# First attention: TensorE's turns issued ahead of its scores; the other attentions fetch q and k by head group

## The chip, the cores and the metric

The kernel runs on one core of a Trainium2 chip. The metric is the device time of one execution in microseconds (us), the median of the runs. All inputs are float32 and lie in the chip's memory at the start; the result must lie there at the end.

## The reference, cut to what matters

A transformer stack of four layers over an input of 4 sequences x 512 tokens x 256 features. Each layer is an attention and a feed-forward part (SwiGLU, a spline lookup, latent experts, experts with a top-2 router):

```
x = x + _L0_attn_ref(_layernorm(x), ...)   # windowed mask, ALiBi, rotary, 8 key/value heads
x = x + _L0_ffn_ref(_layernorm(x), ...)
x = x + _L1_attn_ref(_layernorm(x), ...)   # causal
x = x + _L1_ffn_ref(_layernorm(x), ...)
x = x + _L2_attn_ref(_layernorm(x), ...)   # causal, rotary
x = x + _L2_ffn_ref(_layernorm(x), ...)
x = x + _L3_attn_ref(_layernorm(x), ...)   # no mask
x = x + _L3_ffn_ref(_layernorm(x), ...)
```

Every attention has 16 heads of 16 dimensions: scores q k^T of 512 x 512 for each head and sequence, a softmax over keys, the product with v, and an output projection. The change touches the four attentions alone.

## The kernel before, in words

`build` runs eight stages one after the other, with a barrier between them. `PS` is PSUM, 8 banks of 512 float32 on 128 partitions. SyncE (SP) issues the DMAs, GpSimd (POOL) does small elementwise work.

**The first attention** is `attention_window`. It walks over FULL = 128 steps: 4 sequences (b) x 4 groups of four heads (g) x 2 halves x 4 query blocks of 128. Here a step is called N. On each engine the program is a Python loop over N that was unrolled, so the order in the code is the order on the engine. In step N:

- `scores(N)` (TensorE, L592): two matmuls, one for each of two heads, 128 queries x 448 keys, into banks 2(N mod 2) and 2(N mod 2)+1. It waits for the exponentials of step N-2, since these read the same two banks.
- `minima(N)` (VectorE, L361): for each of the two heads it adds the distance bias in PSUM and takes the row's minimum (the scores are negated).
- `exponentials(N)` (ScalarE, L492): for each of the two heads, exp with that minimum, into the buffer `p`.
- `turn_weights(e)` (TensorE, L602) for the two items e = 2(N-9) and 2(N-9)+1: each item is four 128x128 transposes of `p` of nine steps ago, into bank 4 or 5 (4 + e mod 2). It waits until item e-2 has been copied out of the same bank.
- `keep_turned(e)` copies that bank to `pT`. ScalarE does it (L500), and VectorE for every fifth item (L370, e mod 5 = 2). It stands behind `exponentials(N)` on ScalarE and behind `minima(N)` on VectorE.
- `piece(...)`: in 21 of 32 steps one piece of other work that uses bank 7: layer-norm turns (L556), projections of the next sequence (L568), turning a finished group (L623), turning heads (L630), output projections (L640). The table `plan` says which.
- `values(J)` (TensorE, L616) in every even step from 12 on: probabilities times v, four matmuls.

The last scores are those of step 127; 13 more steps only turn and multiply.

**The other three attentions** are `attention_quads`. q and k are projected with the heads side by side. To spread each head's 16 dimensions over the partitions they go through a buffer in the chip's memory, `spread_scratch`: `store_unit(b, u)` writes unit u (u = 0: q of the head groups 0 and 1, 1: k of the groups 0 and 1, 2 and 3: the same for the groups 2 and 3) in three DMAs of 256 KB, and `fetch_unit(b, u)` reads it back into `q` or `k` in two DMAs of 512 KB, 64 partitions each (L866). The semaphore `spread[u]` counts them. All stand on SP in the order store 0, store 1, fetch 0, fetch 1, store 2, store 3, fetch 2, fetch 3. TensorE's `scores(t)` (L1200) is the first reader: it computes scores for the row maxima only (VectorE, L975), 16 tiles for each group of heads, and it waits before a tile that is the first of groups 0 and 1, or of 2 and 3, until both units have landed. The first attention already fetches by group (L256, L259): four DMAs of 192 KB for each group.

Of the kernel before, what the change touches and what calls it, by code (L numbers as in the profile page):

```python
# [5 lines left out]
F32 = mybir.dt.float32  # L6
# [11 lines left out]
TB = S // P  # L18
# [5 lines left out]
NG = H // GH  # L24
# [94 lines left out]
def attention_window(nc, tag, X, cst, PS, scr, weights, rope, scale, dist, slopes, bias):  # L119
# [4 lines left out]
    NU = 3  # L124
    WC = 2 * (D + VD)
    STEPS = 2 * TB * NG
    FULL = NB * STEPS
# [4 lines left out]
    with ExitStack() as ctx:  # L132
# [3 lines left out]
        sem = ctx.enter_context(stage_semaphores(nc, tag))  # L136
# [9 lines left out]
        q, k = sb("q", [P, RING, 2, S], R32), sb("k", [P, RING, 2, S], R32)  # L146
# [19 lines left out]
        wrote = [sem(f"wrote{u}") for u in range(NU)]  # L166
        spread = [sem(f"spread{g}") for g in range(NG)]
# [15 lines left out]
        def piece_at(N):  # L183

            kind, ahead, i = plan.get(N % STEPS, ("none", 0, 0))
            b = N // STEPS + ahead
            return (kind, b, i) if 0 <= b < NB else ("none", 0, 0)

        def previous_piece(N):
            return next((x for x in (piece_at(n) for n in range(N - 1, -1, -1)) if x[0] != "none"), ("values", 0, 0))  # L190
# [29 lines left out]
        with nc.Block() as block:  # L220
# [325 lines left out]
            def _(pe):  # L546
# [35 lines left out]
                def scores(N):  # L582
                    b, n = N // STEPS, N % STEPS
                    g, half, qt = n // 8, n % 8 // TB, n % TB
                    slot = (NG * b + g) % RING
                    if n % 8 == 0:
                        pe.wait_ge(spread[g], 64 * (b + 1))
                    if N >= 2:
                        pe.wait_ge(exp_done, 2 * (N - 1))
                    for a in range(2):  # L590
                        rows = slice(64 * a, 64 * a + 48)
                        pe.matmul(PS[:, 2 * (N % 2) + a, 0:KW], q[rows, slot, half, qt * P:(qt + 1) * P],  # L592
                                  k[rows, slot, half, GLOB:S], start=True, stop=True).then_inc(s_done, 1)

                def turn_weights(e):

                    gg, kt, i = e // (4 * GH), e % (4 * GH) // GH, e % GH
                    pe.wait_ge(exp_done, 16 * gg + (8 if i < 2 else 16))
                    if e >= 2:
                        pe.wait_ge(*turned_item(e - 2))  # L600
                    for qt in range(TB):
                        mm = pe.transpose(PS[:, 4 + e % 2, qt * P:(qt + 1) * P],  # L602
                                          p[:, GH * (gg % 2) + i, qt, kt * P:(kt + 1) * P], ident)
                    mm.then_inc(pt_done, 1)
# [39 lines left out]
                def piece(kind, b, i, before):  # L644
                    if kind == "none":
                        return
                    pe.wait_ge(*freed(before))
                    if kind == "group":
                        turn_group(b, i)
                    elif kind == "turn":  # L650
                        turn(b, i, 7)
                    elif kind == "project":
                        project(b, i, 7)
                    elif kind == "values":
                        values_of(b)
                    elif kind == "heads":
                        turn_heads(b, i)
                    else:
                        outputs(b, i)
# [16 lines left out]
                pe.wait_ge(xT_done, 2 * KC)  # L676
                pe.wait_ge(sin_done, NU)
                for N in range(END):
                    if N < FULL:
                        scores(N)  # L680
                    for e in (2 * (N - LAG), 2 * (N - LAG) + 1):
                        if 0 <= e < ITEMS:
                            turn_weights(e)
                    piece(*piece_at(N), previous_piece(N))
                    if N % 2 == 0 and 0 <= (N - 12) // 2 < ITEMS // GH:
                        values((N - 12) // 2)
# [7 lines left out]
def attention_quads(nc, tag, X, Y, cst, PS, scr, filled, weights, masks=None, rope=None, bias=None, scrambled=False):  # L694
# [4 lines left out]
    NU = 4  # L699
# [5 lines left out]
    STEPS = 2 * TB * NG  # L705
    TILES_ = 2 * STEPS
    LEAD = 24
    FULL = NB * STEPS
    SCALE = HD ** -0.5
    with ExitStack() as ctx:  # L710
# [3 lines left out]
        sem = ctx.enter_context(stage_semaphores(nc, tag))  # L714
# [34 lines left out]
        unit_high = [sem(f"unit_high{u}") for u in range(NU)]  # L749
        unit_low = [sem(f"unit_low{u}") for u in range(NU)]  # L750
        wrote = [sem(f"wrote{u}") for u in range(NU)]
        spread = [sem(f"spread{u}") for u in range(NU)]
        v_done, va_done = sem("v_done"), sem("va_done")
        s_done, max_done, split_done = sem("s_done"), sem("max_done"), sem("split_done")
        m_done, mT_done, ma_done, mb_done = sem("m_done"), sem("mT_done"), sem("ma_done"), sem("mb_done")
# [72 lines left out]
        with nc.Block() as block:  # L828
            @block.sync
            def _(sp):  # L830
                o = KC * WC
                sp.wait_ge(filled, 16 * 2 * NU)
                if bias is not None:
                    sp.dma_start(bb[:, :], bias.rearrange("(a n) -> a n", a=1).broadcast_to([P, D])
                                 ).then_inc(loaded_bias, 16)
                sp.dma_start(wqk_in, weights[:, 0:o]).then_inc(loaded_qk, 16)
                if rope is not None:
                    sp.dma_start(tabs[:, :, :].rearrange("p a b -> p (a b)"), rope[:, :]).then_inc(loaded_tab, 16)
                sp.dma_start(wv_in, weights[:, o:o + KC * D]).then_inc(loaded_v, 16)
                if causal:  # L840
                    sp.dma_start(masks_in, masks[:, :]).then_inc(loaded_masks, 16)
                sp.dma_start(wo[:, :, :].rearrange("p a b -> p (a b)"),
                             weights[:, o + KC * D:o + KC * D + NC * D]).then_inc(loaded_o, 16)

                def store_unit(b, u):

                    par = b % 2
                    if b >= 2:
                        sp.wait_ge(spread[u], 32 * (b - 1))
                    sp.wait_ge(unit_high[u], b + 1)  # L850
                    for place in ((0, 1) if u % 2 else (0, 3)):
                        sp.dma_start(scr[par, u, place, :, :, :].rearrange("d l c -> (d l) c"),
                                     high[:, u, :].bitcast(F32)).then_inc(wrote[u], 16)
                    sp.wait_ge(unit_low[u], b + 1)
                    sp.dma_start(scr[par, u, 3 if u % 2 else 1, :, :, :].rearrange("d l c -> (d l) c"),
                                 low[:, u, :].bitcast(F32)).then_inc(wrote[u], 16)

                def fetch_unit(b, u):

                    par = b % 2  # L860
                    sp.wait_ge(wrote[u], 48 * (b + 1))
                    if b >= 2 and u == 0:
                        sp.wait_ge(st_done, STEPS * (b - 1))
                    dst = k if u % 2 else q
                    for a in range(2):
                        sp.dma_start(dst[64 * a:64 * a + 64, par, 4 * (u // 2):4 * (u // 2) + 4, :].bitcast(F32),  # L866
                                     scr[par, u, :, :, 4 * a:4 * a + 4, :].rearrange("k d l c -> (k d) l c")
                                     ).then_inc(spread[u], 16)

                for b in range(NB):  # L870
                    store_unit(b, 0)
                    store_unit(b, 1)
                    fetch_unit(b, 0)
                    fetch_unit(b, 1)
                    store_unit(b, 2)
                    store_unit(b, 3)
                    fetch_unit(b, 2)
                    fetch_unit(b, 3)

            @block.gpsimd  # L880
            def _(pool):
# [274 lines left out]
            def _(pe):  # L1156
# [32 lines left out]
                def scores(t):  # L1189

                    gg, qt, half, a = tile_of(t)
                    b, g = gg // NG, gg % NG
                    pair, kw, rows = 2 * g + half, (qt + 1) * P if causal else S, slice(64 * a, 64 * a + 64)
                    if t % (8 * TB) == 0:
                        pe.wait_ge(spread[g // 2 * 2], 32 * (b + 1))
                        pe.wait_ge(spread[g // 2 * 2 + 1], 32 * (b + 1))
                    if t >= 2:
                        pe.wait_ge(max_done, t - 1)
                    ps = PS[:, 4 + a, :]
                    mm = pe.matmul(ps[:, 0:kw], q[rows, b % 2, pair, qt * P:(qt + 1) * P], k[rows, b % 2, pair, 0:kw],  # L1200
                                   start=True, stop=not causal)
                    if causal:
                        pe.matmul(ps[:, kw - P:kw], half_masks[rows, 0, 0, :], half_masks[rows, 1, 0, :],  # L1203
                                  start=False, stop=False)
                        mm = pe.matmul(ps[:, kw - 64:kw], half_masks[rows, 0, 1, :], half_masks[rows, 1, 1, 64:P],  # L1205
                                       start=False, stop=True)
                    mm.then_inc(s_done, 1)
# [1310 lines left out]
```

## Time and profile before

| | us |
|---|---|
| median of 3 runs | 2176.14 |
| lowest and highest run | 2170.74, 2186.18 |
| the profiled execution | 2171.83 |
| its span in the trace | 2170.0 |
| TensorE busy | 1694.2 (78%) |
| VectorE busy | 1176.7 (54%) |
| ScalarE busy | 937.5 (43%) |
| GpSimd busy | 365.6 (17%) |
| DMA | 138.86 MB, 64 GB/s over the span |

The span is the time from the first to the last instruction of the trace; 1.83 us of the execution lie outside it. Busy times of engines overlap, and no engine is busy all the time, so where the time goes is read stage by stage, from the timeline and from what ended each wait. The first attention lies from 46 to 449 us of the span; the first score matmuls of the other three attentions start at 644.3, 1087.6 and 1684.3 us.

### The profile page before, as it was taken

To read this page: it belongs to the slowest core of one execution; us is meant where nothing else is said; L and a number is where in the kernel's file an instruction comes from. 1 tells how busy PE (TensorE), PEld (TensorE's weight loads), DVE (VectorE), ACT (ScalarE), POOL (GpSimd) and SP (SyncE) were. 2 spreads that over 40 slices of the span, in tenths; PEclk is the share of its full clock that TensorE was granted. 3 is DMA by queue.
4 is the path that set the end of the run, shared out by engine and by line. 5 is a ranking of instruction groups with operands and counts; after the bars stand their busy time and mean duration, and the time that the engine had idled before them with its cause. 6 is when DMAs were issued, how large, how long until landed. Compare 5 with 4: busy or idle time off the path is not lost. (4 is left out here: it accounts for less than half of the span.)

```text
span 2170.0 us, 30921 instructions
## 1 busy us (share of the span) xinstructions
PE 1694.2 (78%) x11334; PEld 1050.3 (48%) x11342; DVE 1176.7 (54%) x2681; ACT 937.5 (43%) x1452; POOL 365.6 (17%) x466
## 2 busy tenths in 40 slices
PE   3889898859968999801389999579996899997676
PEld 2445454548855555501255555356665344443543
DVE  2566656543235665489556656242223677774555
ACT  1667778733223544400124445233332356564422
POOL 4120200012323212020322230000001412200000
PEclk8799999989977999955669999769998799999588
DMA  6232230010044335010334541100003345220101
GB/s 206 55 75 55 59 85 4 1 58 0 0 141 108 95 94 137 1 45 0 110 104 105 137 116 22 67 0 0 0 0 91 103 105 136 71 66 22 45 0 39
DMA packets 49297, 138.86 MB, mean 64 GB/s; under 512 B 7169, under 2 KB 12682, under 8 KB 42130
## 3 DMA queue, kind: packets, MB, share of 16 engines
q1 hardware_dynamic: 49170, 137.17, 23.3%
q8 instruction: 80, 1.31, 0.3%
q14 instruction: 47, 0.39, 0.1%
HBM read 87.86 MB, written 51.38 MB: 64 GB/s over the span
## 5 line engine op out<-in xcount | busy, mean ns | idle before, releaser
L975 DVE TENSOR_REDUCE a_mx<-PS 128x1 f32<-128x512 f32 (+3 forms) x768 | 395.9, 554 | 208.8 <-PE PS L1205 132.3
L1146 ACT ACTIVATE a_pT<-PS 128x1024 f32<-128x1024 f32 (+3 forms) x384 | 308.0, 810 | 217.0 <-PE PS L1229 149.3
L1200 PE MATMUL PS<-a_k,a_q 64*128 64x512 f32 (+3 forms) x768 | 236.2, 443 | 59.0 <-DMA a_k<-spread_scratch 28.8
L361 DVE CUSTOM_DVE_ANT_0 PS<-PS,a_dist 128x448 f32<-128x448 f32 x256 | 155.0, 649 | 89.2 <-PE PS L592 88.3
L1220 PE MATMUL PS<-a_q,a_k 64*128 64x512 f32 (+3 forms) x768 | 177.9, 448 | 14.8 <-DVE a_q L980 6.1
L602 PE MATMUL PS<-cst,a_p 128*128 128x128 f32 x1024 | 146.9, 286 | 50.5 <-ACT a_pT L500 45.9
L492 ACT ACTIVATE a_p<-PS,a_negm 128x448 f32<-128x448 f32 (+1 forms) x256 | 152.7, 633 | 77.2 <-DVE a_negm L361 76.4
L1243 PE MATMUL PS<-a_pT,a_va 128*32 128x512 f32 (+3 forms) x1536 | 170.2, 516 | 5.7 <-ACT a_raw L1102 5.7
L1200 PEld LDWEIGHTS PS<-a_k,a_q 64*128 64x128 f32 x768 | 112.5, 202 | 104.6 <-DVE a_mx L975 66.8
L602 PEld LDWEIGHTS PS<-cst,a_p 128*128 128x128 f32 x1024 | 113.4, 145 | 87.2 <-ACT a_p L492 60.7
L1220 PEld LDWEIGHTS PS<-a_q,a_k 64*128 64x128 f32 x768 | 78.8, 192 | 111.1 <-issue 82.7
L500 ACT ACTIVATE a_pT<-PS 128x512 f32<-128x512 f32 x205 | 114.0, 599 | 9.0 <-PE PS L602 8.2
L1918 DVE SCALAR_TENSOR_TENSOR f_acc<-PS,f_gb,f_acc 128x128 f32<-128x128 f32 x144 | 40.6, 345 | 115.5 <-PE PS L2018 115.4
L1954 ACT ACTIVATE f_hid<-PS,f_b 128x512 f32<-128x512 f32 x84 | 57.7, 687 | 77.3 <-PE PS L2009 75.5
L1080 ACT ACTIVATE a_q<-PS 16x1024 fp32r<-16x1024 f32 x48 | 48.7, 1014 | 96.0 <-PE PS L1251 95.6
L1203 PE MATMUL PS<-a_half_masks 64*128 64x128 bf16 x512 | 90.0, 243 | 0.0
L2018 PEld LDWEIGHTS PS<-f_w,f_hid 128*128 128x128 f32 x672 | 80.1, 192 | 15.3 <-issue 14.3
L2009 PE MATMUL PS<-f_lat,f_w 128*128 128x512 f32 x168 | 82.8, 608 | 0.0
L2018 PE MATMUL PS<-f_w,f_hid 128*128 128x128 f32 x672 | 80.2, 275 | 0.0
L592 PE MATMUL PS<-a_k,a_q 48*128 48x448 f32 x256 | 62.9, 489 | 14.8 <-DMA a_k<-window_scratch 9.7
L1205 PE MATMUL PS<-a_half_masks 64*128 64x64 bf16 x512 | 74.4, 200 | 0.0
L1174 PE MATMUL PS<-a_xnT,a_w_highqk 128*128 128x512 f32 x128 | 58.8, 459 | 17.1 <-DVE a_x_low L1029 9.4
(337 smaller groups left out, 3262.9 us busy)
## 6 DMA issues: line engine op xcount, KB each, us to landing
spread_scratch<-a_high SPq DMA_DIRECT2D x96, 256.0 KB, 2.5
a_q<-spread_scratch SPq DMA_DIRECT2D x48, 512.0 KB, 6.6
a_k<-spread_scratch SPq DMA_DIRECT2D x48, 512.0 KB, 9.3
spread_scratch<-a_low SPq DMA_DIRECT2D x48, 256.0 KB, 3.9
window_scratch<-a_high SPq DMA_DIRECT2D x24, 256.0 KB, 2.2
a_q<-window_scratch SPq DMA_DIRECT2D x32, 192.0 KB, 5.3
a_k<-window_scratch SPq DMA_DIRECT2D x32, 192.0 KB, 6.2
window_scratch<-a_low SPq DMA_DIRECT2D x12, 256.0 KB, 2.0
```

The lines of the kernel that those rows point to most:

```text
L361: dve.tensor_tensor_reduce(PS[:, bank, 0:KW], PS[:, bank, 0:KW], dt_[:, off:off + KW], float(slopes[2 * pair + a]), 3e38, ALU.add, ALU.min ...
L492: act.activation(p[p0:P, GH * (gg % 2) + i, qt, 0:KW], PS[p0:P, bank, 0:KW], ACT.Exp, bias=negm[p0:P, bank:bank + 1], scale=-1.0).then_inc ...
L500: act.activation(pT[:, J % 2, i, :], PS[:, 4 + e % 2, :], ACT.Copy).then_inc(turned_act, 1)
L602: mm = pe.transpose(PS[:, 4 + e % 2, qt * P:(qt + 1) * P], p[:, GH * (gg % 2) + i, qt, kt * P:(kt + 1) * P], ident)
L975: dve.tensor_reduce(mx[:, gg % 2, qt, 2 * half + a:2 * half + a + 1], PS[:, 4 + a, 0:kw], AX.X, ALU.max).then_inc(max_done, 1)
L1146: act.activation(pT[:, N // 2 % 2, N % 2, :, q0:S], PS[:, 2 * (N % 2):2 * (N % 2) + 2, q0:S], ACT.Exp, scale=SCALE).then_inc(exp_done, 1)
L1200: mm = pe.matmul(ps[:, 0:kw], q[rows, b % 2, pair, qt * P:(qt + 1) * P], k[rows, b % 2, pair, 0:kw], start=True, stop=not causal)
L1203: pe.matmul(ps[:, kw - P:kw], half_masks[rows, 0, 0, :], half_masks[rows, 1, 0, :], start=False, stop=False)
L1220: mm = pe.matmul(PS[:, 2 * half + a, q0:S], k[rows, b % 2, pair, kt * P:(kt + 1) * P], q[rows, b % 2, pair, q0:S], start=True, stop=not ca ...
L1243: mm = pe.matmul(PS[BLK * i:BLK * i + BLK, 6, q0:S], va[:, b % 2, kt, GH * g + i, :], pT[:, J % 2, i // 2, i % 2, q0:S], start=(kt == 0), ...
L2009: pe.matmul(PS[:, n % 2, :], w1[:, n, :], lat[:, :], start=True, stop=True).then_inc(h_done, 1)
L2018: mm = pe.matmul(PS[:, 2 + e % 2, k * P:(k + 1) * P], hid[:, e % 2, j, k * P:(k + 1) * P], w2[:, first[e] + j, :], start=(j == 0), stop=(j ...
```

## The change

On TensorE in `attention_window`, the two turns of a step now stand ahead of its scores. No instruction is added or removed there. In `attention_quads`, q and k are fetched by group of heads: four DMAs of 256 KB for each group in place of two of 512 KB for each unit; the groups 0 and 1 are fetched when both units 0 and 1 are in the scratch buffer, and TensorE waits for one group at a time.

```diff
@@ attention_window, tensor
                 for N in range(END):
-                    if N < FULL:
-                        scores(N)
                     for e in (2 * (N - LAG), 2 * (N - LAG) + 1):
                         if 0 <= e < ITEMS:
                             turn_weights(e)
+                    if N < FULL:
+                        scores(N)
                     piece(*piece_at(N), previous_piece(N))
@@ attention_quads
-        spread = [sem(f"spread{u}") for u in range(NU)]
+        spread = [sem(f"spread{g}") for g in range(NG)]
@@ store_unit
                     if b >= 2:
-                        sp.wait_ge(spread[u], 32 * (b - 1))
+                        for g in (u // 2 * 2, u // 2 * 2 + 1):
+                            sp.wait_ge(spread[g], 64 * (b - 1))
@@
-                def fetch_unit(b, u):
-
-                    par = b % 2
-                    sp.wait_ge(wrote[u], 48 * (b + 1))
-                    if b >= 2 and u == 0:
-                        sp.wait_ge(st_done, STEPS * (b - 1))
-                    dst = k if u % 2 else q
+                def fetch_group(b, g):
+
+                    par, tile = b % 2, g // 2 * 2
+                    if g % 2 == 0:
+                        sp.wait_ge(wrote[tile], 48 * (b + 1))
+                        sp.wait_ge(wrote[tile + 1], 48 * (b + 1))
+                    if b >= 2:
+                        sp.wait_ge(st_done, STEPS * (b - 2) + 8 * (g + 1))
                     for a in range(2):
-                        sp.dma_start(dst[64 * a:64 * a + 64, par, 4 * (u // 2):4 * (u // 2) + 4, :].bitcast(F32),
-                                     scr[par, u, :, :, 4 * a:4 * a + 4, :].rearrange("k d l c -> (k d) l c")
-                                     ).then_inc(spread[u], 16)
+                        first = 4 * a + 2 * (g % 2)
+                        for u, dst in ((tile, q), (tile + 1, k)):
+                            sp.dma_start(dst[64 * a:64 * a + 64, par, 2 * g:2 * g + 2, :].bitcast(F32),
+                                         scr[par, u, :, :, first:first + 2, :].rearrange("k d l c -> (k d) l c")
+                                         ).then_inc(spread[g], 16)
@@ attention_quads, tensor, scores(t)
-                    if t % (8 * TB) == 0:
-                        pe.wait_ge(spread[g // 2 * 2], 32 * (b + 1))
-                        pe.wait_ge(spread[g // 2 * 2 + 1], 32 * (b + 1))
+                    if t % (4 * TB) == 0:
+                        pe.wait_ge(spread[g], 64 * (b + 1))
```

In the program that this makes, TensorE's order in the first attention changes in every step from 9 to 127. Before, at a place in the first sequence (L602 turns, L592 scores, L616 values, L623 and L630 pieces):

```order
L616 MATMUL PS<-a_pT,a_va 32x512 x4
L592 MATMUL PS<-a_k,a_q 128x448 x2
L602 MATMUL PS<-cst,a_p 128x128 x8
L592 MATMUL PS<-a_k,a_q 128x448 x2
L602 MATMUL PS<-cst,a_p 128x128 x8
L623 MATMUL PS<-cst,a_raw 128x128 x4
L616 MATMUL PS<-a_pT,a_va 32x512 x4
```

Now, on TensorE at the same place:

```order
L616 MATMUL PS<-a_pT,a_va 32x512 x4
L602 MATMUL PS<-cst,a_p 128x128 x8
L592 MATMUL PS<-a_k,a_q 128x448 x2
L602 MATMUL PS<-cst,a_p 128x128 x8
L592 MATMUL PS<-a_k,a_q 128x448 x2
L623 MATMUL PS<-cst,a_raw 128x128 x4
L616 MATMUL PS<-a_pT,a_va 32x512 x4
```

The scores of a step moved behind its eight transposes; pieces and values keep their places.

On SP, at the start of each of the other attentions, the order before was (L852 and L855 stores, L866 fetches):

```order
L852 DMA spread_scratch<-a_high 128x512 x2
L855 DMA spread_scratch<-a_low 128x512
L866 DMA a_q<-spread_scratch 64x2048 x2
L866 DMA a_k<-spread_scratch 64x2048 x2
L852 DMA spread_scratch<-a_high 128x512 x2
L855 DMA spread_scratch<-a_low 128x512
```

And on SP now (L853 and L856 are the same stores, L870 the fetches):

```order
L853 DMA spread_scratch<-a_high 128x512 x2
L856 DMA spread_scratch<-a_low 128x512
L870 DMA a_q<-spread_scratch 64x1024
L870 DMA a_k<-spread_scratch 64x1024
L870 DMA a_q<-spread_scratch 64x1024
L870 DMA a_k<-spread_scratch 64x1024
L870 DMA a_q<-spread_scratch 64x1024
L870 DMA a_k<-spread_scratch 64x1024
L870 DMA a_q<-spread_scratch 64x1024
L870 DMA a_k<-spread_scratch 64x1024
L853 DMA spread_scratch<-a_high 128x512 x2
L856 DMA spread_scratch<-a_low 128x512
```

Eight half-size fetches stand where four stood; the first four of them are group 0.

## Rows read from the trace of the kernel before

**Rows 1.** Page, costliest groups: line engine op x count | busy, mean ns | idle before, releaser.

```profile
L361 DVE CUSTOM_DVE_ANT_0 PS<-PS,a_dist 128x448 f32<-128x448 f32 x256 | 155.0, 649 | 89.2 <-PE PS L592 88.3
...
L602 PE MATMUL PS<-cst,a_p 128*128 128x128 f32 x1024 | 146.9, 286 | 50.5 <-ACT a_pT L500 45.9
L492 ACT ACTIVATE a_p<-PS,a_negm 128x448 f32<-128x448 f32 (+1 forms) x256 | 152.7, 633 | 77.2 <-DVE a_negm L361 76.4
```

**Rows 2.** Timeline of TensorE, 232 to 238 us: start, us, engine line op.

```profile
232.09 0.47 PE L592 MATMUL PS<-a_k,a_q 48*128 48x448 f32 x2
232.49 1.09 PE L602 MATMUL PS<-cst,a_p 128*128 128x128 f32 x8
233.52 0.47 PE L592 MATMUL PS<-a_k,a_q 48*128 48x448 f32 x2
235.17 1.12 PE L602 MATMUL PS<-cst,a_p 128*128 128x128 f32 x8 [1.19 <-ACT a_pT L500]
236.12 0.60 PE L630 MATMUL PS<-cst,a_at 128*128 128x128 f32 x4
236.65 1.07 PE L616 MATMUL PS<-a_pT,a_va 128*32 128x512 f32 x8
237.65 0.47 PE L592 MATMUL PS<-a_k,a_q 48*128 48x448 f32 x2
```

**Rows 3.** Timeline of VectorE and ScalarE, the same stretch.

```profile
232.60 0.63 DVE L361 CUSTOM_DVE_ANT_0 PS<-PS,a_dist 128x448 f32<-128x448 f32 x1 [0.68 <-PE PS L592]
...
233.32 1.21 ACT L492 ACTIVATE a_p<-PS,a_negm 128x448 f32<-128x448 f32 x2 [1.13 <-DVE a_negm L361]
234.44 1.08 ACT L500 ACTIVATE a_pT<-PS 128x512 f32<-128x512 f32 x2
235.39 1.17 ACT L492 ACTIVATE a_p<-PS,a_negm 128x448 f32<-128x448 f32 x2
```

**Rows 4.** Timeline of TensorE: scores and turns of steps 9 and 10.

```profile
72.47 0.74 PE L592 MATMUL PS<-a_k,a_q 48*128 48x448 f32 x2 [0.35 <-ACT a_p L492]
73.15 1.97 PE L602 MATMUL PS<-cst,a_p 128*128 128x128 f32 x8
75.05 0.74 PE L592 MATMUL PS<-a_k,a_q 48*128 48x448 f32 x2
```

**Rows 5.** Timeline of TensorE: the scores of step 127, the last.

```profile
418.92 0.47 PE L592 MATMUL PS<-a_k,a_q 48*128 48x448 f32 x2
```

**Rows 6.** Timeline of VectorE in step 10, TensorE at the lower clock.

```profile
75.82 0.63 DVE L361 CUSTOM_DVE_ANT_0 PS<-PS,a_dist 128x448 f32<-128x448 f32 x1 [1.26 <-PE PS L592]
```

**Rows 7.** Windows: stretch, busy of PE PEld DVE ACT POOL, clock, DMA share, GB/s.

```profile
46.00:72.00 26.00, 13.09 (x34) 5.53 (x34) 14.48 (x41) 11.05 (x20) 12.57 (x16) 0.63 0.58 136
...
73.00:82.00 9.00, 8.91 (x39) 7.29 (x38) 4.71 (x15) 7.20 (x13) 0.00 (x0) 0.50 0.00 0
...
330.00:420.00 90.00, 73.05 (x518) 43.35 (x517) 54.08 (x158) 70.60 (x130) 0.00 (x0) 1.00 0.00 1
```

**Rows 8.** Waits: who waited for whom, us in total, times, longest.

```profile
PE PS L1200 <- DMA a_k<-spread_scratch: 28.8, 3, 10.5
```

**Rows 9.** Timeline of SP and TensorE at the start of the second attention.

```profile
631.56 1.13 SPq L866 DMA_DIRECT2D a_q<-spread_scratch  x2
633.97 1.08 SPq L866 DMA_DIRECT2D a_k<-spread_scratch  x2
...
644.30 0.80 PE L1200 MATMUL PS<-a_k,a_q 64*128 64x512 f32 x2 [9.39 <-DMA a_k<-spread_scratch]
```

**Rows 10.** The first attention's start: first fetch issued by SP, first scores.

```profile
39.06 0.33 SPq L256 DMA_DIRECT2D a_q<-window_scratch  x1
...
46.01 0.74 PE L592 MATMUL PS<-a_k,a_q 48*128 48x448 f32 x2 [9.73 <-DMA a_k<-window_scratch]
```

**Rows 11.** Page, DMA issues: KB each, median us from issue to landing.

```profile
a_q<-spread_scratch SPq DMA_DIRECT2D x48, 512.0 KB, 6.6
a_k<-spread_scratch SPq DMA_DIRECT2D x48, 512.0 KB, 9.3
```

More of the change, by code:

```diff
@@ L872, in _ @@
                     store_unit(b, 1)
-                    fetch_unit(b, 0)
-                    fetch_unit(b, 1)
+                    fetch_group(b, 0)
+                    fetch_group(b, 1)
                     store_unit(b, 2)
                     store_unit(b, 3)
-                    fetch_unit(b, 2)
-                    fetch_unit(b, 3)
+                    fetch_group(b, 2)
+                    fetch_group(b, 3)
             @block.gpsimd
```

## The prediction

> **What bounds the kernel now.** I read the stage table of the timeline first: eight stages with barriers, so each edit pays only in its own stage, and nothing can pass from one stage to the next. Then the costliest groups: in the first attention ScalarE sat idle 77.2 us ahead of its exponentials, ended nearly always by VectorE's minima; VectorE sat idle 89.2 us ahead of the minima, ended by the scores; TensorE sat idle 50.5 us ahead of the turns, ended by ScalarE's copies of earlier turns [rows 1]. No engine is full; they wait for one another in a ring. So the question is the ring's length, and that is read from the timeline of one pair of steps.
>
> An even step starts with its scores at 232.09 and its turns at 232.49; the odd step's scores follow at 233.52, at once. The odd step's turns wait 1.19 us for ScalarE's copies and start at 235.17; then come a piece (236.12), the values (236.65) and the next even step's scores at 237.65 [rows 2]. On the other engines: minima from 232.60, exponentials from 233.32, copies of the turns from 234.44, and the odd step's exponentials from 235.39, without idle time, since its scores had been issued early [rows 3]. Two steps took 237.65 - 232.09 = 5.56 us, 2.78 a step. What the reader is to see: the odd step's scores stand ahead of the turns that wait, so the way scores, minima, exponentials of one step runs beside the way copies, turns of the step before. That overlap is what makes 2.78 possible.
>
> Over the whole stage, the scores of step 9 (the first step with turns) start at 72.47 [rows 4], and those of step 127, the last, at 418.92 [rows 5]: 346.4 us for 118 steps, 2.94 each.
>
> **The change, part one: turns ahead of scores.** It adds and removes no instruction. Follow the waits in the new order. The turns of step N+1 go to banks 4 and 5 and wait until the turns of step N are copied out. ScalarE's copies of step N stand behind its exponentials of step N. Those need the minima of N, these the scores of N, and the scores of N now stand behind the turns of N on TensorE, which works in order. So turns, scores, minima, exponentials, copies, turns of the next step form one ring, with a single step in it, and nothing overlaps. Its length, link by link, at the full clock:
>
> - scores' start to minima's start: 232.60 - 232.09 = 0.51 [rows 2, 3]
> - minima's start to exponentials' start: 233.32 - 232.60 = 0.72 [rows 3]
> - exponentials' start to the copies' start: 234.44 - 233.32 = 1.12 [rows 3]
> - copies' start to the next turns' start (the first copy must be out, the second follows while the first item is turned): 235.17 - 234.44 = 0.73 [rows 2, 3]
> - turns' start to the next instruction of TensorE, now the scores: 236.12 - 235.17 = 0.95 [rows 2]; where the turns do not wait in between, it is about 1.03, as 233.52 - 232.49 shows.
>
> The sum is 4.03 us. I take 0.1 off (3.92): one item in five is copied by VectorE, which is free by then, and where that is the first of a pair, in one step of five, ScalarE's own copy is over some 0.45 us sooner (by the 1.08 us of two copies, which pipeline, against 0.60 for one). What else a step does is hidden in this ring: TensorE is idle from the end of the scores, about 0.4 us after their start, until the turns, 0.51 + 0.72 + 1.12 + 0.73 = 3.08 us after their start; a piece like L630 (0.53 us, 236.65 - 236.12) and the values (1.00 us, 237.65 - 236.65) fit [rows 2]. A projection and the values together fill it about exactly; I give that nothing. ScalarE's and VectorE's pieces fall into waits of 1.7 us and more.
>
> So 118 steps x 3.92 = 462.6 us at the full clock. The first nine steps have no turns and the last thirteen no scores: unchanged.
>
> **The clock.** At the start of this stretch TensorE ran at 1.2 GHz: the granted clock was 0.50 from 73 to 82 us while TensorE was busy 8.91 of 9 us [rows 7]; from 330 to 420 us it was 1.00 at 73.05 busy us of 90 [rows 7]. A step at 1.2 GHz: turns to next scores take 75.05 - 73.15 = 1.90 instead of 0.95 to 1.03 [rows 4], scores to minima 75.82 - 75.05 = 0.77 instead of 0.51 [rows 4, 6]. The new ring holds both in full: 3.92 + 0.9 + 0.26 is about 5.2 us with a little more for the second copy's wait, 1.3 more a step. Before, the lower clock lasted about ten microseconds of the stretch after step 9, four steps. Busy time per step stays (73.05 us in 90 is 2.26 a step at 2.78), so the busy share falls from 0.81 to 2.26 / 3.92 = 0.58. The nearest stretch with so little is 46 to 72 us: busy 13.09 of 26, clock 0.63 [rows 7], but that has waits of several us, where here no idle gap is over 2.7. I take 12 steps of 118 at the lower clock: 12 x 1.3 = 16 us. Ends: 4 steps (5 us) and all of them (153 us).
>
> Here a rule speaks against the change. By the Trainium skill ("TensorE: Matmul & The Clock Gate", Part 4, on transposes by TensorE), transposes do not count as activity for the clock the way other matmuls do. The row from 73 to 82 us, where only turns and scores ran and the clock stayed at 0.50, agrees. By that rule the activity that counts would be thinner still in the new order, and the all-low end of the range nearer; that is the clock rival below.
>
> Sum of part one: 462.6 + 16 - 346.4 = +132 us.
>
> **Part two: fetch by group.** TensorE waited for k's landing three times, once at each of the other attentions' starts, 28.8 us in all [rows 8]; in later sequences it never did, so only the starts can gain. In the second attention q's fetches were issued at 631.56, k's at 633.97, and the scores began at 644.30 [rows 9], 10.3 us after k's issue. Now nothing is issued before both units are stored, so q's head start of 2.4 us goes, and four DMAs of 256 KB are issued from 633.97 on. The nearest case is the first attention's: its first fetch of group 0 (four DMAs, 768 KB in all) was issued at 39.06 and the scores began at 46.01, 6.95 us later [rows 10]. With 1 MB I take 7.7 us (0.75 more for the further 256 KB, at the rate of the fetches there), so 641.7 in place of 644.3: 2.6 us for each attention, 8 us for three. Ends: nothing (the eight DMAs of both groups share the engines, and group 0 lands with group 1), and 12 us. Group 1 has 16 tiles' time to land; the stores of units 2 and 3 stand behind four more issues, about 2.2 us later by 1.13 us for two [rows 9], and their readers come 32 tiles later.
>
> A DMA of 512 KB landed after 6.6 to 9.3 us at the median [rows 11]. The Trainium skill ("DMA: Bandwidth & Descriptors", Bandwidth) advises DMAs of 1 MiB and more, so halving them would cost bandwidth. By that rule part two could be worth nothing; the first attention's start shows that several small DMAs in flight together land quickly, so I keep 8.
>
> **Sum**, against the profiled execution of 2171.83 us (the median of the runs, 2176.14, is 4 us higher): 2171.8 + 132 - 8 = 2296 us, slower by about 5.5% of the median. What a measurement can tell from no change is about 1%, 22 us.
>
> **The rivals.**
> - The clock falls for much of the stage. For it: the busy share of 0.58, and the row from 73 to 82. Against it: once up, the clock stayed at 1.00 for 90 us, and a busy stretch of turns, scores, piece and values of 2.5 us or more recurs in each pair of steps. If 60 of 118 steps are low: 60 x 1.3 = 78 us in place of 16, 2358 us; if all, 2433.
> - It gives time back: the single ring does not form, since some slack that I do not see lets the exponentials of a step go ahead. Turns issued first would then end ScalarE's idle time before copies, and the wait of 1.19 us per pair of steps would move off the scores' way. The price would be at best that wait in half of the pairs, 30 x 1.19 = 35 us, with part two 43: 2129 us. It decides from the point where minima of step N are done before ScalarE has ended the copies of N-1. Against it: already now in even steps ScalarE waits 1.13 us for the minima [rows 3], and these steps' scores come later in the new order, not sooner.
> - The reordering costs nothing, because ScalarE's total work (about 2.2 us a step) or VectorE's sets the pace: then only part two shows, 2164 us. Against it: ScalarE idled 77.2 us before the exponentials [rows 1].
> - Part of the ring is shorter: the second copy, or the copies by VectorE, let TensorE start earlier, 3.5 us a step in place of 3.92: 118 x 0.42 = 50 us less, 2246 us. I hold it within the forecast's tail.
>
> **How the numbers follow.** Forecast 0.76 (own range 2246 to 2345), clock 0.15, given back 0.03, no cost 0.06. Only the last two end at or under no change; the no-cost case lies within 1%. Leaving out the given-back and no-cost cases and the far end of the clock rival, the range is 2250 to 2375. Faster 0.03, within 1% 0.06, slower 0.91.
>
> **What would show it.** In the new profile: scores of steps 9 and 127 some 460 to 490 us apart instead of 346; in the steady state one ring of 3.9 us with idle time ahead of the minima, of the exponentials and of the turns in every step, not in every second; ScalarE's idle time before the exponentials up from 77 to about 200 us; the busy time of every group unchanged at the full clock; the starts of the other three attentions some 2.6 us shorter. I am wrong if exponentials follow the copies without idle time in odd steps still, or if the clock's row shows long stretches at 0.5.

## The result, and the profile after

The changed kernel takes 2364.95 us (median of 4 runs, 2360.94 to 2367.3), the kernel before 2177.51 us; the ratio is 1.086, with a 95% interval of 1.081 to 1.090. It is slower, as forecast, and by 69 us more than the forecast of 2296; the time lies 10 us inside the upper end of the range. The profiled execution took 2363.09 us (span 2361.3, against 2170.0), so 191 us are to be found.

First the ends of the stages. The first DMA of the stage after the first attention, in the timeline of SP of the kernel before and, below it, of the changed one:

```profile
449.86 0.36 SPq L1373 DMA_DIRECT2D f_wi<-in_f_in  x1
...
639.00 0.36 SPq L1376 DMA_DIRECT2D f_wi<-in_f_in  x1
```

So 639.00 - 449.86 = 189.1 of the 191 us arise in the first attention. The first DMAs of the later stages tell the rest, stage by stage, in us before and after: 166.5 and 166.7, 309.9 and 311.7 (second attention), 123.4 and 123.3, 340.8 and 336.7 (third), 263.8 and 266.3, 345.9 and 345.9 (fourth); the last stage to the end of the span, 169.9 and 171.7.

Within the first attention, these rows of the timeline of TensorE, at both ends, answer to [rows 4, 5]; the scores of step 9 are those at 72.53, the scores of step 127 those at 606.55:

```profile
70.63 1.97 PE L602 MATMUL PS<-cst,a_p 128*128 128x128 f32 x8
72.53 0.74 PE L592 MATMUL PS<-a_k,a_q 48*128 48x448 f32 x2
75.88 1.94 PE L602 MATMUL PS<-cst,a_p 128*128 128x128 f32 x8 [2.61 <-ACT a_pT L500]
77.75 0.74 PE L592 MATMUL PS<-a_k,a_q 48*128 48x448 f32 x2
...
606.55 0.47 PE L592 MATMUL PS<-a_k,a_q 48*128 48x448 f32 x2
```

606.55 - 72.53 = 534.0 us for 118 steps, 4.53 each, where it was 346.4 and 2.94. The page's costliest groups answer to [rows 1]:

```profile
L361 DVE CUSTOM_DVE_ANT_0 PS<-PS,a_dist 128x448 f32<-128x448 f32 x256 | 155.4, 649 | 317.9 <-PE PS L592 317.9
L602 PE MATMUL PS<-cst,a_p 128*128 128x128 f32 x1024 | 179.2, 329 | 152.0 <-ACT a_pT L500 135.0
...
L492 ACT ACTIVATE a_p<-PS,a_negm 128x448 f32<-128x448 f32 (+1 forms) x256 | 155.0, 632 | 268.8 <-DVE a_negm L361 268.7
```

The work of VectorE's minima and of ScalarE's exponentials is nearly unchanged (155.0 and 155.4 us, 152.7 and 155.0 us). What grew is idle time, on all three engines: VectorE ahead of the minima from 89.2 to 317.9, ScalarE ahead of the exponentials from 77.2 to 268.8, TensorE ahead of the turns from 50.5 to 152.0. That is how a ring looks: everyone waits for the one ahead and nobody is the bound. The one busy time of these groups that grew much is TensorE's (the turns from 286 to 329 ns in the mean); these are the same transposes at a lower mean clock, as the windows below show.

The ring itself, at the full clock, in the timeline of one step of the changed kernel. It begins with the scores; the piece of this step is a projection (L568):

```profile
271.32 0.47 PE L592 MATMUL PS<-a_k,a_q 48*128 48x448 f32 x2
...
271.72 1.98 PE L568 MATMUL PS<-a_xT,a_wqk 128*128 128x512 f32 x4
...
271.82 0.63 DVE L361 CUSTOM_DVE_ANT_0 PS<-PS,a_dist 128x448 f32<-128x448 f32 x1 [1.76 <-PE PS L592]
...
272.55 1.22 ACT L492 ACTIVATE a_p<-PS,a_negm 128x448 f32<-128x448 f32 x2 [2.37 <-DVE a_negm L361]
...
273.67 1.07 ACT L500 ACTIVATE a_pT<-PS 128x512 f32<-128x512 f32 x2
...
274.40 1.11 PE L602 MATMUL PS<-cst,a_p 128*128 128x128 f32 x8 [0.69 <-ACT a_pT L500]
...
275.44 0.47 PE L592 MATMUL PS<-a_k,a_q 48*128 48x448 f32 x2
```

Read it downwards: scores, minima 0.50 later, exponentials 0.73, copies 1.12, turns 0.73, the next scores 1.04: 4.12 us. The idle times in brackets show that the minima, the exponentials and the turns each waited for the link before; the projection fits into TensorE's wait and leaves 0.69 us of it. In [rows 2, 3] the odd step's scores at 233.52 lay ahead of the waiting turns; here nothing does.

The windows of the stretch, the changed kernel (columns as in [rows 7]):

```profile
73.00:607.00 534.00, 386.11 (x1942) 213.37 (x1940) 207.93 (x601) 260.18 (x469) 35.52 (x36) 0.79 0.13 30
250.00:280.00 30.00, 25.62 (x144) 13.89 (x141) 15.57 (x43) 16.17 (x30) 3.81 (x3) 1.00 0.35 79
...
140.00:150.00 10.00, 7.13 (x30) 3.96 (x29) 5.45 (x14) 4.00 (x7) 2.77 (x4) 0.50 0.88 158
```

The granted clock of the stretch is 0.79 (0.97 before, from 73 to 419 us): it alternated between its two levels, 1.2 and 2.4 GHz, with 1.00 from 250 to 280 us and 0.50 from 140 to 150. TensorE's idle gaps in the stretch were up to 2.61 us long, some 35 of them over 2 us; in the kernel before only one was over 2 us (2.17).

The second part, fetch by group: the wait for k's landing fell from 28.8 us [rows 8] to

```profile
PE PS L1203 <- DMA a_k<-spread_scratch: 19.2, 3, 6.9
```

At the second attention's start the first fetch was issued at 823.03 and the scores began at 830.42, 7.39 us later (timeline of SP and TensorE):

```profile
823.03 0.49 SPq L870 DMA_DIRECT2D a_q<-spread_scratch  x1
...
830.42 0.80 PE L1203 MATMUL PS<-a_k,a_q 64*128 64x512 f32 x2 [6.14 <-DMA a_k<-spread_scratch]
```

### The profile page after: what moved, and what is told of

Read it like the earlier page. It is cut to its first block and busy times, and to the rows that moved or that the text cites. A ratio compares the mean times of both kernels' runs of the same rounds, so it can differ in the third digit from the quotient of the medians.

```text
span 2361.3 us, 31066 instructions
## 1 busy us (share of the span) xinstructions
PE 1796.6 (76%) x11342; PEld 1094.0 (46%) x11342; DVE 1174.6 (50%) x2681; ACT 942.2 (40%) x1452; POOL 365.5 (15%) x466
## 5 line engine op out<-in xcount | busy, mean ns | idle before, releaser
L361 DVE CUSTOM_DVE_ANT_0 PS<-PS,a_dist 128x448 f32<-128x448 f32 x256 | 155.4, 649 | 317.9 <-PE PS L592 317.9
L602 PE MATMUL PS<-cst,a_p 128*128 128x128 f32 x1024 | 179.2, 329 | 152.0 <-ACT a_pT L500 135.0
L492 ACT ACTIVATE a_p<-PS,a_negm 128x448 f32<-128x448 f32 (+1 forms) x256 | 155.0, 632 | 268.8 <-DVE a_negm L361 268.7
L602 PEld LDWEIGHTS PS<-cst,a_p 128*128 128x128 f32 x1024 | 140.0, 169 | 257.2 <-ACT a_p L492 243.9
L616 PE MATMUL PS<-a_pT,a_va 128*32 128x512 f32 x512 | 92.3, 805 | 0.0
L592 PE MATMUL PS<-a_k,a_q 48*128 48x448 f32 x256 | 74.1, 576 | 14.4 <-DMA a_k<-window_scratch 9.6
```

The costliest lines, as they stand in the source:

```text
L361: dve.tensor_tensor_reduce(PS[:, bank, 0:KW], PS[:, bank, 0:KW], dt_[:, off:off + KW], float(slopes[2 * pair + a]), 3e38, ALU.add, ALU.min ...
L492: act.activation(p[p0:P, GH * (gg % 2) + i, qt, 0:KW], PS[p0:P, bank, 0:KW], ACT.Exp, bias=negm[p0:P, bank:bank + 1], scale=-1.0).then_inc ...
L602: mm = pe.transpose(PS[:, 4 + e % 2, qt * P:(qt + 1) * P], p[:, GH * (gg % 2) + i, qt, kt * P:(kt + 1) * P], ident)
L616: mm = pe.matmul(PS[BLK * i:BLK * i + BLK, 6, :], va[:, b % 2, kt, 2 * g + i // 2, :], pT[:, J % 2, i, :], start=(kt == 0), stop=(kt == TB ...
```

## The experiments

**1. The first part alone.** The kernel before, with the turns ahead of the scores.

```diff
                 for N in range(END):
-                    if N < FULL:
-                        scores(N)
                     for e in (2 * (N - LAG), 2 * (N - LAG) + 1):
                         if 0 <= e < ITEMS:
                             turn_weights(e)
+                    if N < FULL:
+                        scores(N)
```

> The change's first part alone: turns ahead of scores in the first attention; the other attentions fetch by unit as in the kernel before. Theory (one ring of turns, scores, minima, exponentials, copies in each step, at a clock that alternates): all of the loss is here; from the scores of step 9 to those of step 127 about 534 us as in the changed kernel (346 before), total about 2367 us, within 6 us of the changed kernel plus 2 to 8 us. Rival (the fetches by group carry part of the loss, by taking DMA or SP time from the first attention's neighbours): total 2340 us or less.

Measured: 2369.5 us (2 runs), ratio 1.089 (1.084 to 1.094). From the scores of step 9 (72.37) to those of step 127 (611.3): 538.9 us, clock 0.77. All of the loss is in the first part; the rival falls.

**2. The second part alone.** Fetch by group as in the changed kernel, TensorE's order in the first attention as before. Only the calls are shown; `fetch_group`, the semaphores and TensorE's wait are those of the diff of the change.

```diff
-                fetch_unit(b, 0)
-                fetch_unit(b, 1)
+                fetch_group(b, 0)
+                fetch_group(b, 1)
```

> The change's second part alone: fetch by group of heads, TensorE's order in the first attention as before. Theory of the prediction: the waits for k's landing at the three starts go from 28.8 to about 20 us and the time falls by 8 us (0.4%). Rival, from the changed kernel's trace, where the second attention took 311.7 us against 309.9 although its wait was shorter: the wait's gain is given back behind it, the time falls by 0 to 3 us or not at all.

Measured: 2167.05 us against 2174.66 (12 and 17 runs), ratio 0.9965 (0.9945 to 0.9984): 7.6 us faster. The wait for k is 20.5 us in its trace, 8.3 less than before. That is the forecast of 8, and more than the rival allowed, though the interval (3.5 to 12 us) does not exclude that some of the shorter wait is given back. Single traces can't settle that: with fetch by group the second attention took 311.7 and 310.9 us, with fetch by unit 309.9 and 309.5; the third 336.7 and 339.6 against 340.8 and 338.7; the fourth 345.9 and 343.0 against 345.9 and 346.1. All three together took 994.3 and 993.5 us against 996.6 and 994.3, so the traces show less gain in these stages than the shorter waits alone would give. That fetch by group saves time is shown; that all of it is saved at the three starts is not.

**3. Cut the ring on the other side.** The changed kernel, with the copies of a step's turns ahead of its exponentials on ScalarE and of its minima on VectorE.

```diff
                 for N in range(END):
-                    if N < FULL:
-                        exponentials(N)
                     for e in (2 * (N - LAG), 2 * (N - LAG) + 1):
                         if 0 <= e < ITEMS and not on_dve(e):
                             keep_turned(e)
+                    if N < FULL:
+                        exponentials(N)
```

and the same exchange of `minima(N)` and `keep_turned(e)` on VectorE.

> The changed kernel, and on ScalarE and VectorE the copies of a step's turns stand ahead of its exponentials and minima. This cuts the ring: the copies of N no longer wait for the scores of N. Ring theory: turns ahead of scores then costs nothing, and a step takes about 2.66 us at the full clock by a replay of the waits with the link durations of the trace: 314 us from the scores of step 9 to those of step 127, against 534 in the changed kernel and 346 before; total about 2140 us. Rival (the order on TensorE itself costs, for instance since turns and scores at the lower clock feed each other whatever ScalarE does): 420 us or more for these 118 steps, total above 2240 us.

Measured: 2141.18 us, ratio 0.984 (0.981 to 0.987): 224 us less than the changed kernel, and 33 us less than the kernel before. The 118 steps took 394.4 - 72.74 = 321.7 us, 2.73 each, 8 us more than the 314 expected, at a clock of 0.99:

```profile
73.00:394.00 321.00, 295.21 (x1937) 171.47 (x1938) 210.20 (x601) 256.88 (x468) 35.64 (x36) 0.99 0.21 50
```

TensorE's order is exactly that of the changed kernel, its work too; what is gone is only the link "copies of N wait for the scores of N". ScalarE's idle time ahead of the exponentials fell from 268.8 us to 39.4:

```profile
L492 ACT ACTIVATE a_p<-PS,a_negm 128x448 f32<-128x448 f32 (+1 forms) x256 | 153.3, 634 | 39.4 <-DVE a_negm L361 37.8
```

**4. The same with TensorE's old order.** As experiment 3, and scores ahead of turns again.

```diff
                 for N in range(END):
+                    if N < FULL:
+                        scores(N)
                     for e in (2 * (N - LAG), 2 * (N - LAG) + 1):
                         if 0 <= e < ITEMS:
                             turn_weights(e)
-                    if N < FULL:
-                        scores(N)
```

> As the run with the copies ahead, but with TensorE's order of before (scores ahead of turns), so that the two orders on TensorE can be compared without the ring. Ring theory: the same within 5 us as with turns ahead (313 against 314 us for the 118 steps by the replay), total about 2140 us. Rival (scores first is better by itself): at least 20 us faster than the run with turns ahead.

Measured: 2138.67 us, ratio 0.982 (0.979 to 0.986); 391.4 - 72.54 = 318.9 us for the 118 steps. The two orders of TensorE, which differ by some 190 us when ScalarE runs exponentials first, differ by 2.5 us here, within their intervals. So TensorE's order by itself costs nothing that these runs can tell; the cost is in the pair of orders. This kernel is also faster than both kernels of the study, by 36 us than the one before. Both kernels with the copies ahead also fetch by group, which experiment 2 puts at 7.6 us; the rest of the 36 fits the stretch, 318.9 in place of 346.4 us.

**5. Shorten the ring.** The changed kernel, with the scores between the two items.

```diff
                     for e in (2 * (N - LAG), 2 * (N - LAG) + 1):
                         if 0 <= e < ITEMS:
                             turn_weights(e)
-                    if N < FULL:
-                        scores(N)
+                        if e % 2 == 0 and N < FULL:
+                            scores(N)
```

> The changed kernel, with the scores of a step between its two turned items: first item, scores, second item. The ring then leaves out the second copy (about 0.5 us) and the second item's transposes (about 0.45 us) for most steps. Ring theory: the replay gives 3.46 us a step at the full clock in place of 3.90, that is 409 us for the 118 steps, and with the clock as low as in the changed kernel some 450 to 480 (534 there, 346 before); total 2280 to 2320 us. Rival (not the ring's length but only whether all scores come ahead of all turns decides): 534 us as in the changed kernel, or 346 as before.

Measured: 2293.47 us (2 runs), ratio 1.054 (1.041 to 1.066); 537.0 - 72.66 = 464.3 us for the 118 steps, 3.94 each, clock 0.85. The loss is neither all nor nothing: it goes with what lies in the ring, as the ring theory says. The steps that ran wholly at the full clock show it without the clock: 65 of them here took 3.67 us in the mean, 44 in the changed kernel 4.10. The 3.46 us that was expected is 0.2 too short.

**6. Keep the ring and hold the clock up.** The changed kernel, with one or two more matmuls behind the scores of most steps; their results are not used.

```diff
+                def filler(N):
+                    pe.wait_ge(exp_done, 2 * N)
+                    for a in range(2 if N % 2 else 1):
+                        pe.matmul(PS[:, 2 * ((N + 1) % 2) + a, 0:384], wqk[:, 0, 0:P], wqk[:, 0, 0:384], start=True, stop=True)
...
                     if N < FULL:
                         scores(N)
+                    if LAG <= N < FULL - 1 and (N % 2 or N < 12 or piece_at(N)[0] in ("none", "group", "heads", "turn")):
+                        filler(N)
```

> The changed kernel, and behind the scores of a step TensorE runs one or two further matmuls (float32, 128 x 384) on constant weights into the banks that the next step's scores overwrite; the results are not used. They lie in the 2.7 us in which TensorE otherwise waits for the copies, and keep it active. Theory (the ring is 3.9 us at the full clock, and the rest of the loss, 534 - 463 = 71 us, is the alternating clock): granted clock 0.95 or more in the stretch, 118 steps in 460 to 490 us, total 2295 to 2320 us, faster than the changed kernel although it does more work. Rival (the ring's links are longer than read, the clock is a side effect): clock up, and the 118 steps still at 520 us or more.

Measured: 2317.13 us (2 runs), ratio 1.064 (1.053 to 1.076). The scores of step 9 began at 71.72 and those of step 127 at 564.3: 492.6 us, 4.17 a step, which is 3 us above the 460 to 490 that were expected; the total lies inside its range. The windows of this run:

```profile
72.00:564.00 492.00, 423.58 (x2277) 229.53 (x2278) 209.26 (x601) 259.97 (x469) 35.56 (x36) 1.00 0.14 33
```

The clock came up within the first steps: the eight transposes of a step (L607 in this kernel) took 1.97 us at 69.83 and 1.23 at 78.92. The added matmuls (L598) were busy for 139.8 us. TensorE's busy time is only 37 us above the changed kernel's, because everything else ran at the higher clock; the stretch is 41 us shorter and the kernel 48 us faster than the changed one. So part of the loss is the low clock.

The added matmuls also lengthen some steps, so the 4.17 us are not the ring alone. The projection step of the changed kernel shown above took 4.12 us, and TensorE waited 0.69 us before its turns. Such a step here:

```profile
97.39 0.47 PE L592 MATMUL PS<-a_k,a_q 48*128 48x448 f32 x2
97.79 1.56 PE L598 MATMUL PS<-a_wqk 128*128 128x384 f32 x4
99.19 1.88 PE L568 MATMUL PS<-a_xT,a_wqk 128*128 128x512 f32 x4
100.90 1.04 PE L607 MATMUL PS<-cst,a_p 128*128 128x128 f32 x8
```

The next scores began at 101.87, 4.48 us after 97.39: with the added work ahead of the projection TensorE no longer waits and itself sets the length. All 14 steps of 4.47 to 4.49 us in this trace have added matmuls and a projection or an output projection. The changed kernel has 44 steps wholly at the full clock. 26 of them differ by at most 0.01 us from the same step here; the other 18 are shorter there, nearly all of them steps with such a piece. Together the 44 took 180.5 us there and 189.7 here. So at least 9 of the 492.6 us belong to the added matmuls, and the ring at the full clock, the added work left out, is by this estimate at most 483 us, 4.1 a step. That splits the loss of 188 us into at most 483 - 346 = 137 us for the ring and at least 534 - 483 = 51 us for the low clock; the raw difference, 534.0 - 492.6 = 41, understates the clock.

## Why the prediction was right, and where it was off

**The ring: right.** The prediction said that turns, scores, minima, exponentials and copies would form one ring with a single step in it. The changed kernel's timeline shows it link by link, experiment 3 removes it by cutting one link on another engine, experiment 5 shortens it. The links as read from the old trace (0.51, 0.72, 1.12, 0.73, 0.95 to 1.03) are 0.50, 0.73, 1.12, 0.73, 1.04 in the new one.

**The ring's length: nearly 0.2 us a step too short.** The prediction took 3.92 us; the 44 steps of the changed kernel at the full clock took 4.10 in the mean. Two terms of the sum were mis-sized. The last link was taken as 0.95, from a step in which the turns are followed by a piece, although the other value that the prediction gave, 1.03, is the right one: 0.09 a step. And the pieces and values were given nothing. In the odd steps, which have no values, that holds, with a projection too: none of those 44 took over 4.13 us. But of the even ones, which have them, most took 4.20 to 4.53; with a projection or output projection and the values behind it, 4.34, since these together do not fit into the 3.08 us. That is the other 0.09; the other even steps were not followed link by link. The deduction of 0.1 for VectorE's copies was about right: 4.12 against 3.63 us in one step of five. Together about 118 x 0.18 = 21 us.

**The clock: the right mechanism, 12 steps where it was about 43.** The length of a step wholly at 1.2 GHz came out as said (5.2 us forecast; the step from 72.53 to 77.75 took 5.22), which is 1.1 above the 4.12 of the full clock, not 1.3. But the share did not: the clock came up and fell again all along, mean 0.79. That is some 225 of the 534 us at the lower level, the time of about 43 such steps, and it cost about 51 us by the estimate of experiment 6 where 16 was taken. The prediction argued that no idle gap would be over 2.7 us and so the clock would mostly stay up. The gaps were as short as said (2.61 us at most), and it fell nevertheless, over 30 times. It had also read "once up, the clock stayed at 1.00" from 330 to 420 us alone; in the same trace of the kernel before, the stretches 100 to 110, 120 to 130, 130 to 140 and 255 to 265 us were each granted 0.83.

**How much was luck.** The forecast case had 2246 to 2345 us as its own range, and 2365 lies outside it; only the range widened for the clock rival holds it. That rival's figure, 2358, is much nearer than the forecast's 2296, but not because it was right: it took 60 low steps at a price of 1.3 where there were about 43 at 1.1, and the longer ring and what came out longer in the other stages made up the difference.

**Do transposes count for less?** The rule of the Trainium skill on transposes by TensorE ("TensorE: Matmul & The Clock Gate", Part 4), which the prediction weighed against the change, is not tested by itself here. In experiment 6 a few ordinary matmuls beside the same transposes held the clock at 1.00, but they added busy time as well. Experiment 3 has the same transposes and no added matmul, and its clock was 0.99; it was at 0.50 from 70 to 77 us and at 1.00 from 78 to 88, after nothing but scores and turns from 67.3 us on. So the rule is not needed to explain the low clock; what changed from experiment 3 to the changed kernel is the waiting.

**The rest.** The second part was worth 7.6 us alone, forecast 8; first issue to first scores 7.39 us, forecast 7.7. That the second figure came so near is partly luck: the 0.75 us for the further 256 KB was said to be at the rate of the first attention's fetches, but these moved 180 to 221 GB/s in the trace of the kernel before (40 to 46 us), which gives 1.2 to 1.5 us, and measured it was 7.39 - 6.95 = 0.44. In the one trace of the changed kernel the three attentions gained only 2 us net, and the other stages, from the first attention's tail (32.5 in place of 30.9 us) to the last stage, are 6 us longer in sum; single traces of the same stage differ by as much. ScalarE's idle time ahead of the exponentials went to 268.8 us, not to the 200 that the prediction named as its sign, as the steps were longer than it took them. Step by step: 21 (ring) + 35 (clock) + 6 (second part in this trace) + 6 (stages), which is, but for rounding, the 67 us between 2363 and 2296. The first two rest on the estimate of experiment 6; only their sum, 534.0 - 462.6 - 16 = 55 us, is measured.

**The rivals.** "It gives time back" and "costs nothing" fell with the first result, and "part of the ring is shorter" with the links: a step takes 4.10 us at the full clock, not 3.5. Of the first, one thing was true in another place: ScalarE's idle time ahead of the exponentials can be had back, though by moving the copies and not the turns.

## What to carry to other kernels

When two engines each run two kinds of work in a fixed order, draw the waits of one step as a graph over both orders before exchanging anything: moving an instruction behind a waiting one on its own engine costs the whole chain that hangs on it, if the wait in turn depends on that chain one step earlier. The cure need not be on the engine where the order was changed; issuing the copies ahead of the exponentials made both orders of TensorE equal and, with the fetch by group (0.35% of it), the kernel 1.8% faster than it was. And once engines wait for each other, count TensorE's lower clock into the sum: here it was about 51 of 188 us. When work is added to show what a wait costs, look at each step for what the added work costs itself.

## What the runs showed of the hardware that had not been expected

TensorE's granted clock alternated between 0.5 and 1.0 through 534 us in which it was busy 386 us and idle for at most 2.61 us at a time: it fell over 30 times, and its mean was 0.79. In the kernel before (298.5 of 346 us busy) it fell four times, mean 0.97; in experiment 3 (295.2 of 321 us), with the same instructions on TensorE in the same order as in the changed kernel, it did not fall after its first rise, mean 0.99. Adding 169 matmuls whose results nobody reads kept it at 1.00 and made the kernel 48 us faster (2364.95 to 2317.13), although they lengthened some steps.
